# Attention of a windowed transformer block regrouped: small matmuls in quarters of the array, scores of three heads by row groups, half chunks of 1176 score columns

## What is computed

```python
h = _layer_norm(x, ln1_g, ln1_b)
h = jnp.roll(h, (-SHIFT, -SHIFT), axis=(1, 2))
xw = _window_partition(h, WS).reshape(-1, N, C)           # N = 49, C = 48
qkv = xw @ w_qkv + b_qkv                                  # 6 heads of 8
attn = jnp.einsum('whnd,whmd->whnm', q, k)                # q scaled
attn = attn + rel_bias[None]                              # + mask of the shift
attn = jax.nn.softmax(attn, axis=-1)
o = jnp.einsum('whnm,whmd->whnd', attn, v)
o = o @ w_proj + b_proj                                   # windows and roll undone
x = shortcut + o
y = _layer_norm(x, ln2_g, ln2_b)                          # goes to the convolutions
```

## Time and profile before

| | us |
|---|---|
| median of 3 runs | 3709.49 (3706.65 to 3709.59) |
| the profiled execution | 3707.4 |
| its span, first to last instruction | 3705.6 |
| attention, 512 to 2616 us | 2104 |
| attention per chunk (128) | 16.4 |

### The profile page before, as it was taken

One profiled execution on the slowest core, in us unless ns is written; L12 is line 12 of the kernel. 1 busy time (PEld: TensorE's weight loads), 2 busy tenths in 40 slices (PEclk: granted clock), 3 DMA queues, 4 the chain that ended last, 5 costly groups with the idle time before them and its releaser, 6 DMA issues. The chain is left out here.

```text
span 3705.6 us, 94419 instructions
## 1 busy us (share of the span) xinstructions
PE 3445.4 (93%) x31796; PEld 2390.5 (65%) x31796; DVE 2853.4 (77%) x4885; ACT 2389.6 (64%) x4324; POOL 2047.7 (55%) x2188
## 2 busy tenths in 40 slices
PE   6898879999999999999999999999599999999998
PEld 3566557667667667667667667666366666666665
DVE  4543457777777777777777777777599999999998
ACT  3432337777777777777777777777366666666665
POOL 1110146666666666666666666666255555555554
PEclk8898789999999999999999999999799999999999
DMA  4331021111111111111111111111566665666663
GB/s 113 105 103 44 22 61 40 38 35 39 38 34 39 38 35 39 38 34 39 38 34 39 38 34 39 38 34 37 82 109 113 109 108 99 105 105 112 111 104 62
DMA packets 235789, 230.18 MB, mean 62 GB/s; under 512 B 118064, under 2 KB 230704, under 8 KB 232624
## 3 DMA queue, kind: packets, MB, share of 16 engines
q1 hardware_dynamic: 235696, 229.14, 30.6%
HBM read 151.26 MB, written 77.76 MB: 62 GB/s over the span
## 5 line engine op out<-in xcount | busy, mean ns | idle before, releaser
L614 POOL TENSOR_TENSOR kex<-ks,cw 112x294 f32<-112x294 f32 x1024 | 734.2, 750 | 232.8 <-ACT ks L866 232.8
L674 PE MATMUL ps_s<-kex,qbd 112*98 112x294 f32 x2048 | 592.4, 411 | 0.0
L1256 POOL TENSOR_TENSOR ya_lo<-ya,ya_hi 128x464 fp32r<-128x464 f32 x224 | 284.4, 1270 | 310.1 <-DVE ya_hi L1426 210.4
L1013 DVE TENSOR_TENSOR s<-ps_s,bias 98x294 f32<-98x294 f32 x1024 | 434.9, 454 | 14.1 <-PE ps_s L674 2.2
L674 PEld LDWEIGHTS ps_s<-kex,qbd 112*98 112x98 f32 x2048 | 318.4, 165 | 165.3 <-issue 80.2
L889 ACT ACTIVATE pt<-ps_t 98x588 f32<-98x588 f32 x512 | 338.1, 660 | 120.2 <-PE ps_t L685 114.5
L1025 DVE TENSOR_REDUCE mx<-s 98x12 f32<-98x588 f32 x512 | 390.8, 763 | 13.2
L1262 POOL TENSOR_TENSOR hid_a_lo<-hid_a,hid_a_hi 128x448 fp32r<-128x448 f32 x224 | 298.1, 1331 | 183.9 <-ACT hid_a_hi L1353 183.9
L1029 DVE TENSOR_TENSOR s<-s,mx 98x588 f32<-98x588 f32 x384 | 388.5, 1012 | 13.1
L685 PEld LDWEIGHTS ps_t<-cw,s 98*98 98x98 f32 x3072 | 300.6, 127 | 101.8 <-issue 46.9
L882 ACT ACTIVATE s<-s 98x588 f32<-98x588 f32 x512 | 354.4, 692 | 4.5 <-DVE s L1029 1.4
(11 more groups left out here) (164 smaller groups left out, 7186.2 us busy)
## 6 DMA issues: line engine op xcount, KB each, us to landing
ya<-y_chunks SPq DMA_DIRECT2D x64, 532.9 KB, 6.4
y_chunks<-y SPq DMA_DIRECT2D x256, 76.1 KB, 1.8
xin<-x_chunks SPq DMA_DIRECT2D x256, 73.5 KB, 2.5
xres<-x_chunks SPq DMA_DIRECT2D x256, 73.5 KB, 1.9
x_chunks<-xo SPq DMA_DIRECT2D x256, 73.5 KB, 1.8
out<-xr SPq DMA_DIRECT2D x32, 588.0 KB, 5.4
yb<-y_chunks SPq DMA_DIRECT2D x96, 177.6 KB, 8.1
xr<-x_chunks SPq DMA_DIRECT2D x32, 514.5 KB, 5.7
```

Of the source, the lines that this page charges most:

```text
L614: pool.tensor_tensor(kex[a][:, win, :, :], ks[:, win, :].unsqueeze(1).to_broadcast([PP, HEADS, N]), w("head").unsqueeze(2).to_broadcast([P ...
L674: pe.matmul(ps_s[win % 3][0:2 * N, 0:HN], qbd[a][:, win, :], kex[a][:, win, :, :].rearrange("c h k -> c (h k)"), start=True, stop=True).th ...
L1013: dve.tensor_tensor(s_sb[i][:, k, :], ps_s[win % 3][0:2 * N, 0:HN], bias[:, low, int(win == NWC - 1), :], ALU.add).then_inc(s_biased, 1)
```

## The change

`attention` is rewritten; the rest is word for word the same.

- **Quarters.** Small products use 64 x 64 quarters of the array: `center`, queries, keys and `project` become 4 products each of a 48-row weight and 196 columns (half of the windows of one image); `value_rows` 32 products with 24 moving columns; `values` 48 per half chunk, each one head, 9 moving columns, row half = head group g, column half = image; `outputs` 16 products over 49 rows.
- **Scores** of a half chunk (4 windows) are 16 products: 24 rows (three heads of one image, on one of four row groups of 32) by 147 columns, into the four banks of `ps_s`. `kex` has 3 heads instead of 6.
- **Half chunks.** Bias, maxima and exponential each become 2 instructions per chunk over 1176 columns. The subtraction of each half is split: VectorE takes image 0, GpSimd image 1, 588 columns each.
- **Transposes** are 113 x 113 instead of 98 x 98, 24 per chunk as before. `transposes(n-1, 3)` stands right behind `transposes(n-1, 2)`, and `center2` right behind `transposes(n, 1)`; `center2` now uses `ps_t`.
- **Variances** are one 32-bit product each, of squares that GpSimd makes; ScalarE's squares and the split are gone. The affine step of y moves from ScalarE to GpSimd; the doubled copy of h is gone.
- **DMA.** `xin` and `xres` get 3 more columns by DMAs of their own (12-byte rows); `xres` and `xo` have rows of 224 bytes instead of whole lines: 12 DMAs per chunk.

```diff
             def scores(n, half, a):
+                tiled()
+                pe.wait_ge(kex_set, n * 2 + half + 1)
+                for p in range(2):
+                    for u in range(2):
+                        win = half * NH + p * 2 + u
+                        for g in range(4):
+                            group = slice(32 * g, 32 * g + C // 2)
+                            mm = pe.matmul(ps_s[rows(u, N), g, p * TR * N:(p + 1) * TR * N], q[a][group, win, :],
+                                           kex[a][group, win, :, :].rearrange("c j k -> c (j k)"), start=True, stop=True)
...
+                for p in range(2):
+                    for u in range(2):
+                        for j in range(TR):
+                            for g in range(2):
+                                for img in range(2):
+                                    to = ((p * 2 + u) * TR + j) * VW
+                                    block = (img * NH + p * 2 + u) * TR + j
+                                    mm = pe.matmul(ps_m[rows(img, N), g, to:to + VW], pt[half * 2 + p][rows(g, N), img, j, u, :],
+                                                   vs[a][rows(g, N), half, block, :], start=True, stop=True)
```

More of the change, by code:

```diff
@@ new lines, in center, with variance @@
+            def center(n, a):
+                for img in range(2):
+                    for half in range(2):
+                        px = xin[a][rows(img, C), :, SHIFT + half * HW2:SHIFT + half * HW2 + HW2]
+                        mm = pe.matmul(ps_s[rows(half, BO), 2 + img, 0:HP], w("center")[rows(img, C), rows(img, BO)],
+                                       px.rearrange("c r (w k) -> c w r k", w=NH), start=True, stop=True)
+                mm.then_inc(center_mm, 1)
+            def variance(n):
+                pe.wait_ge(squared, n + 1)
+                pe.matmul(ps_m[0:PP, 0, 0:T2], w("sum"), sq[:, :, :], start=True, stop=True).then_inc(var_mm, 1)
@@ new lines, in value_rows @@
+            def value_rows(n):
+                for img in range(2):
+                    for win in range(NH):
+                        for half in range(2):
+                            for g in range(2):
+                                to = (img * NH + win) * (C // 2)
+                                mm = pe.matmul(ps_s[rows(g, N), half, to:to + C // 2], h[rows(half, C), img, win, :],
+                                               wvs[rows(half, C), g * (C // 2):(g + 1) * (C // 2)], start=True, stop=True)
+                mm.then_inc(v_mm, 1)
@@ L749, in project @@
             def project(n):
+                tiled()
                 pe.wait_ge(ot_set, n + 1)
-                misc(1, w("wp"), ot[:, :, :], proj_mm)
+                for half in range(2):
+                    for img in range(2):
+                        mm = pe.matmul(ps_m[rows(img, C), half, 0:HP], w("wp")[rows(half, C), :],
+                                       ot[rows(half, C), img, :].rearrange("c (w r k) -> c r w k", w=NH, r=WS), start=True, stop=True)
+                mm.then_inc(proj_mm, 1)
@@ L783, in body @@
-                if after:
-                    pe.wait_ge(ln_done, n + 2)
-                    queries(n + 1)
-                transposes(n, 1)
-                scores(n, 3, a)
-                if after:
-                    keys(n + 1)
-                    value_rows(n + 1, 0)
-                values(n, 0, a)
-                if before:
-                    outputs(n - 1, 1 - a)
-                if after:
-                    value_rows(n + 1, 1)
-                transposes(n, 2)
                 if before:
@@ new lines, in packed_attention @@
+        "wvp": both(w_qkv[:, third[2]][:, order]), "wp": both(w_proj[order]),
+        "g1": both(ln1_g), "be1": both(ln1_b), "bq": twice(grouped(b_qkv[third[0]])), "bk": twice(grouped(b_qkv[third[1]])),
+        "bv": both(b_qkv[third[2]][order]), "bp": both(b_proj), "g2": both(ln2_g), "be2": both(ln2_b),
+        "rel": rels, "masked": masks, "center": center, "sum": total,
+        "head": twice(grouped(np.kron(np.tile(np.eye(TR), 2), np.ones((1, HD)))).T), "eps": np.full(PP, EPS, np.float32),
```

717 lines of the change are left out of this document (338 added, 379 removed).

## The result

The changed kernel takes 4858.5 us (median of 4 runs, 4837.5 to 4876.0) against 3709.5 (3706.7 to 3712.0): a ratio of 1.310 [1.304, 1.315]. I had said 3525, at most 3980. Its profiled execution takes 4852.6 us, its span is 4850.8.

The account below looks back on a forecast made before the run. TensorE was taken to bound attention: products 10.1, shape changes 0.45, waits 4.0 us, 14.55 a chunk, 14.9 with small unknowns, against 16.39. Over 128 chunks that saves 190 us: 3525 us, 8-in-10 range 3440 to 3980.

Parts of the forecast that it names:

- The pace of the quarters: TensorE's small products: four quarters work at once, 0.0117 us a record, so 96 `values` records take 1.12 us.
- (a): Rival: row halves bring nothing for tiny products, 0.0233 us a record, 18.25 us a chunk, 3950 us; chance 22%.
- (b): Rival: in-between pace of 0.014 to 0.019 us a record, 3610 to 3790 us; chance 17%.
- (c): Rival: no row concurrency in the long products either, about 21 us a chunk, 4320 us; chance 6%.
- The waits and the list: TensorE's chunk: products 10.1 us, shape changes 0.45, seven new waits 4.0, together 14.55 us.
- the two waits on `ps_t`: TensorE idle while `ps_t` is copied, before `transposes(n-1, 3)` and before `center2`: 1.10 us each.
- The waits before scores: TensorE, before `scores(n, 1)`: waits for ScalarE's copies of queries and keys, 0.23 us.
- for VectorE's step: TensorE, before `variance`: waits for VectorE's `outputs` step of `values(n-1, 0)`, 0.55 us.
- before `values`, `outputs` and `project`: TensorE waits for the transposes' copy, VectorE's step and the copy of `outputs`: 0.36, 0.41 and 0.25 us.
- granted clock 1.00: Expected sign in the attention stage: TensorE's clock stays at the 2.4 GHz level, as before the change.
- Rival (d): Clock falls to 1.2 GHz as TensorE idles 30% of the stage, doubling its 10.1 us: 4500 or more; chance 3%.
- some 20 more wait instructions: TensorE's chunk: without a row of their own; with `tiled()` and small misfits taken as 0.35 us.

Follow-up runs that it names:

- before_idle: Kernel before the change, with one wait more behind each duo's transposes until their result is copied, products unchanged: 4978.6 us.
- after_align: The aligned kernel: changed kernel with only padding waits ahead of TensorE's two attention loops, so each starts on a 16 KB packet and touches 7: 3867.6 us.
- after_split: after_align with the 96 `values` records issued as twice 48 with other work between, and `variance2` moved between two duos' transposes: 3565.1 us.
- after_align_dense: after_align with the quarter products of `values` replaced by large ones of a constant tile, of about equal duration; result not right: 3519.4 us.
- after_rot: Changed kernel with TensorE's two attention loops made one, its turn cut in the wait between `transposes(n-1, 2)` and `(n-1, 3)`: 3826.4 us.
- The reordering: after_align with `transposes(n-1, 2)` moved ahead of the variances and `value_rows` behind `transposes(n, 1)`: 4267.0 us.
- after_split_h: after_align with the `values` records issued as twice 48, but `variance2` left where it was: 3710.9 us.
- after_unroll: Changed kernel with TensorE's loop over chunks written out, other engines keeping theirs: 4361.7 us, ratio 1.179.

## Why the prediction was wrong, point by point

**The pace of the quarters: right.** I took 0.0117 us a record, 1.12 us for `values` with 0.09 for a change of shape. Measured at full clock: 96 records in 710.12 - 708.88 = 1.24 us; 32 of scores in 703.42 - 702.74 = 0.68 (0.52 and a change); `outputs` in 0.51 (0.37 and a change). The row halves do work side by side, so rivals (a), (b) and (c) fall, on which I had put 45%. The Trainium skill's page TensorEngine Tiling (Array Packing), section Instruction Overhead, gives each matmul some 60 cycles. As a limit on the whole stream, which is how I weighed it, this is not borne out: 1.24/96 is 13 ns a record. Within one quarter a record takes 4 x 13 = 52 ns, so about the overhead of a single tile these rows say nothing against it.

**The waits and the list: right in their sum, and that in part by luck.** I had 1.10 us for each of the two waits on `ps_t`, ahead of `transposes(n-1, 3)` and of `center2`. The profile puts 0.75 before each, as its idle time begins only when the modelled end of the transposes is over: L699 starts at 712.48 and again at 713.99, 1.51 us later, of which 0.60 were my 6 transposes, so 0.9; for `center2` it is 1.0. The waits before scores (0.39) and for VectorE's step (0.20 before `variance`) are there. Those that I put before `values`, `outputs` and `project` (0.36, 0.41, 0.25) are not: `project`, for one, starts at 704.70, right behind the transposes. In the terms of my sum the waits come to some 2.7 us and not 4.0. The products took as much more: 6 transposes 704.70 - 703.93 = 0.77 for 0.60, `center2` 708.88 - 708.03 = 0.85 for 0.66, and so on down the list. The two errors cancel, the chunk is 14.61 where the walk gave 14.55, and the kernel with dense `values` takes 3519 where I said 3525. Two terms among the other engines were off as well: with a fixed part of 0.15 us the bias over 1176 columns is 0.15 + 4 x 0.304 = 1.37 us, not 1.29 (it measured 1.38), and VectorE's subtraction beside GpSimd measured 0.79 us, not 1.25. Nothing hung on them.

**The step that failed: "granted clock 1.00".** I carried the clock of the kernel before over to a kernel with other products. Rival (d) named it, with a price of 4500 or more, and I gave it 3%. By its own terms a chunk would be 14.9 + 10.1 = 25.0 us; that 24.9 were measured is partly luck, since some 3 of them are the gap at the turn. Its mechanism (TensorE idle 30% of the time) was only part of it. The runs showed a mean clock of 0.56 in the stage. Idle time counts (`before_idle`: 1.00 to 0.73), but with dense products in place of the quarter `values`, and the same waits, the clock was 1.00 where the aligned kernel has 0.84. What I left out is that the clock depends on the products too. That it is the small part of the array that a quarter product of 9 columns uses is the likely reason, not a shown one.

**What no line of the sum had: the supply of instructions.** I listed "some 20 more wait instructions", and not that the records per chunk double (25329 records of the stage before, 51878 after, both for 128 chunks) and with them the length of the loop, from 846 instructions to 1702 (counted in the traces). That takes the loop from 4 or 5 packets of 16 KB to 8. The page before had 35 instruction packets; nothing in it shows the limit, but the growth of the loop could be counted.

**How the 1334 us between 3525 and 4859 divide.** Placement of the loop 4859 - 3868 = 991, of which 62 x 6.2 = 385 are gaps and the rest is mostly the clock. The clock with the quarter `values`: 3868 - 3519 = 349. Together they are 6 us too many, by which my number lay above the dense kernel's. The aligned kernel's own spread, 3829.7 to 3916.0, moves the border between the first two by some tens of us. The parts are not additive in another order: from `after_split` the placement costs 864.

**Left open.** What exactly the clock weighs is not settled. Low use of the array in a stretch fits `after_align_dense`, `after_rot` and `after_split`; so would the number of short instructions and weight loads in it, and in `after_split` less idle time. A kernel with as many short instructions and a fuller array, or the other way round, was not run. The reordering came with waits of up to 2.5 us, and whether these or the order of the products took the clock to 0.64 is open, as is why `after_split_h` gained only 157 us. Why 8 packets are fetched again and 7 are not was measured at few lengths and placements, no finer. And `after_unroll` takes 4362 us where `after_align` takes 3868, though its waits for issue before scores and `outputs` are only 29.7 and 28.5 us in all from 600 to 3000 us; the rest of the difference is a lower clock, and why it is lower in straight code was not tried.

## What to carry to other kernels

Before cutting products into smaller tiles, count the instructions of the loop and see how many packets of 16 KB it touches; compare the number of instruction packets on the page with that of the program's length, and pad the start of a loop that is just too long. A sum of durations at full clock is only a forecast if the clock stays. Small products set between large ones, and into waits, were the order that kept it here. Look at the waits after every reordering: two here moved a wait and didn't remove it. When a change makes the work shorter and the kernel slower, look first at the granted clock and at waits for issue.

## What the runs showed of the hardware that I had not expected

- TensorE keeps a loop of up to 7 packets of instructions (1702 instructions, 49 packets fetched in the whole run) and fetches one that touches 8 anew in each turn (588; 8.9 a turn), with a gap of 6.2 us on average. 310 long fulfilled waits as padding made this kernel 20% faster.
- Four quarters of the array together take a record each 13 ns (96 in 1.24 us), a weight load of 49 columns included; a product of 32-bit data is two records.
- With TensorE busy for 88% of the time and 2.0 us idle a chunk the mean granted clock was 0.84 (`after_align`), with 87% and 1.9 us it was 1.00 (`after_align_dense`). What differs is the products of `values`: 96 quarter records, or 4 over the whole array.
- Four waits more per chunk cost the kernel before 1270 us, 9.9 us per chunk: some 3.8 us of idle time, and the rest because the clock fell to 0.73 with them.
